# Attention: the logarithm of each row's sum joins its maximum in the by-key pass

## The reference

```
h = layernorm(x, gamma1, beta1)
q, k, v = h @ Wq + bq, h @ Wk + bk, h @ Wv + bv
scores = q @ k.T / sqrt(32), masked above the diagonal
context = softmax(scores) @ v
attention = context @ Wo + bo
```

## Time and profile before

| | |
|---|---|
| time, median of 3 runs | 1732.72 us (1732.4 to 1734.18) |
| profiled execution, first to last instruction | 1732.7 us |
| TensorE busy | 1657.8 us, 96% |
| VectorE busy | 1174.8 us, 68% |
| ScalarE busy | 977.3 us, 56% |
| GpSimd busy | 437.3 us, 25% |
| TensorE in the chain that ended last | 77% |
| mean granted TensorE clock | 0.980 |

### The profile page before, as it was taken

One profiled execution on the slowest core, in us unless ns is written; L12 is line 12 of the kernel. 1 busy time (PEld: TensorE's weight loads), 2 busy tenths in 40 slices (PEclk: granted clock), 3 DMA queues, 4 the chain that ended last, 5 costly groups with the idle time before them and its releaser, 6 DMA issues.

```text
span 1732.7 us, 27454 instructions
## 1 busy us (share of the span) xinstructions
PE 1657.8 (96%) x9416; PEld 1331.5 (77%) x9416; DVE 1174.8 (68%) x2758; ACT 977.3 (56%) x2258; POOL 437.3 (25%) x670
## 2 busy tenths in 40 slices
PE   6799988899999999999999899999999999999999
PEld 4688766667676777767777568888999999999998
DVE  6799775777777767685867737767565656565643
ACT  5788753777676767676767654634242424242422
POOL 5788530323132313223231212010101010101010
PEclk8899998999999999999999989999999999999999
DMA  7122233443444434344433524576646464646451
GB/s 308 51 97 79 92 122 97 99 99 93 116 100 117 99 97 125 81 123 99 99 88 85 183 104 170 209 279 241 243 170 243 170 243 170 244 170 243 171 195 67
DMA packets 61826, 254.81 MB, mean 147 GB/s; under 512 B 10580, under 2 KB 15956, under 8 KB 45944
## 3 DMA queue, kind: packets, MB, share of 16 engines
q1 hardware_dynamic: 61688, 253.06, 44.8%
HBM read 153.93 MB, written 48.23 MB: 117 GB/s over the span
## 4 chain that ended last, share of the span: by engine, by line
PE 77%; DVE 9%; ACT 4%; DMA 4%; SPq 2%; issue 2%; POOL 1%; DVEq 0%; POOLq 0%; ACTq 0%
PE psum L82 21%; PE psum L83 20%; PE psum L84 20%; PE psum L1632 4%; PE psum L1660 3%; PE psum L1613 3%; SPq L920 2%; DVE psum L1165 2%; PE psum L1538 2%; ACT psum L1408 1%; DMA k_stack<-k_samples 1%; DMA k_raw<-in_w_in 1%; DVE k_tokens L1216 1%; DVE k_samples L1206 1%; PE psum L1556 1%
## 5 line engine op out<-in xcount | busy, mean ns | idle before, releaser
L1408 ACT ACTIVATE psum<-psum,b_mx 128x512 f32<-128x512 f32 (+3 forms) x512 | 259.1, 507 | 199.4 <-DVE b_mx L1165 197.2
L1165 DVE CUSTOM_DVE_ANT_0 psum<-psum,b_mask 128x512 f32<-128x512 f32 (+3 forms) x512 | 244.4, 504 | 141.8 <-PE psum L1613 141.0
L2489 ACT ACTIVATE k_act<-k_stack_f,k_smalls 128x512 f32<-128x512 f32 x112 | 81.0, 723 | 336.5 <-DVE k_stack_f L2277 336.5
L1418 ACT ACTIVATE k_exps<-psum 128x512 f32<-128x512 f32 (+1 forms) x384 | 204.1, 533 | 20.6 <-PE psum L1632 18.7
L1632 PE MATMUL psum<-k_stack 98*128 98x512 f32 (+3 forms) x512 | 159.3, 353 | 16.5 <-ACT k_exps L1418 16.2
L2130 POOL TENSOR_SCALAR k_result<-k_result,k_pb 128x512 f32<-128x512 f32 x32 | 59.9, 1886 | 448.4 <-DVE k_result L2196 448.4
L2256 DVE TENSOR_TENSOR k_act_lo<-k_act,k_act_hi 128x512 fp32r<-128x512 f32 x112 | 77.3, 691 | 130.9 <-ACT k_act_hi L2492 130.8
L1613 PE MATMUL psum<-k_stack 96*128 96x512 f32 (+3 forms) x512 | 150.1, 335 | 2.5 <-ACT psum L1408 2.5
L82 PE MATMUL psum<-k_act_hi,k_w_hi 128*128 128x512 f32 x384 | 150.9, 393 | 0.6 <-DVE k_act_lo L2256 0.6
L83 PE MATMUL psum<-k_act_lo,k_w_hi 128*128 128x512 f32 x384 | 150.7, 392 | 0.0
L84 PE MATMUL psum<-k_act_hi,k_w_lo 128*128 128x512 f32 x384 | 150.4, 392 | 0.0
(11 more groups left out here) (368 smaller groups left out, 4563.7 us busy)
## 6 DMA issues: line engine op xcount, KB each, us to landing
k_stack<-w_factors SPq DMA_DIRECT2D x35, 1792.0 KB, 8.0
k_stack<-k_samples SPq DMA_DIRECT2D x384, 128.0 KB, 2.4
k_weights<-w_factors SPq DMA_DIRECT2D x17, 1792.0 KB, 7.6
x<-k_tokens SPq DMA_DIRECT2D x10, 1024.0 KB, 4.1
k_tokens<-x SPq DMA_DIRECT2D x8, 1024.0 KB, 5.0
d<-k_result SPq DMA_DIRECT2D x32, 256.0 KB, 2.5
k_raw<-x SPq DMA_DIRECT2D x8, 1024.0 KB, 4.8
k_raw<-d SPq DMA_DIRECT2D x8, 1024.0 KB, 7.0
```

The source lines that it names most:

```text
L1165: last = dve.tensor_tensor_reduce(got, got, mask[:, S - width:S], -INV_SQRT_DH, -2.0 * MASKED, ALU.add, ALU.min, mx[n % 2][:, h, t:t + 1])
L1408: act.activation(sc(n, u)[:, at:at + width], sc(n, u)[:, at:at + width], ACT.Exp, bias=mx[n % 2][:, h, t:t + 1], scale=-1.0, accum_out=sum ...
L1418: act.activation(exps[n % 2][:, h, at:at + width], by_key(n, u)[:, 0:width], ACT.Exp, scale=INV_SQRT_DH).then_inc(k_act, 1)
L2489: act.activation(act_f[:], whole_tile, ACT.Gelu, bias=small(smalls, "b1", 2 * pair % M + second)).then_inc(pair_gelu, 1)
```

## The change

The row sum's logarithm is subtracted from `mx` once the exponentials by query of a half are done. The by-key pass then gives exp(score - maximum - log(sum)), which is the softmax itself, and the context needs no scaling. ScalarE takes the logarithm of a half (`log_sums`, 128x8), VectorE subtracts it (`shift_rows`, 128x8), and only then does TensorE transpose the half. The second half's transpose and its split move from step 1 to step 2, on VectorE behind `qk_out`. The reciprocal, its spread, its four transposes, the piece "bc" and `over_sums` are gone. ScalarE rounds the context to its high part straight from PSUM, in step 6 instead of 7, and VectorE takes the low part from the PSUM bank in step 7. The transpose of the first half waits for that low part, since it writes the same bank.

```
@@ bank_uses: "bc" is gone from each list @@
-    bc = [("bc", *divmod(n - 2, G), "dve")] if 0 <= n - 2 < GROUPS else []
@@ VectorE @@
-        def invert(n):
-            dve.wait_ge(e_act, exps_until(n, UNITS - 1))
...
-            dve.reciprocal(recs[:], sums[n % 2][:]).then_inc(rec_set, 1)
-
-        def over_sums(n):
...
-            dve.tensor_tensor(ctx_at(n), ctx_at(n), pj(name), ALU.mult).then_inc(pj_dve, 1)
+        def shift_rows(n, half):
+
+            dve.wait_ge(log_set, 2 * n + half + 1)
+            both = two_heads(mx[n % 2], half)
+            dve.tensor_tensor(both, both, two_heads(logs, half), ALU.subtract).then_inc(shift_set, 1)
 
         def ctx_low(n):
             dve.wait_ge(ch_set, n + 1)
-            dve.tensor_tensor(low_at(n), ctx_at(n), ch[:, n % G, :].bitcast(F32), ALU.subtract).then_inc(cl_set, 1)
+            dve.tensor_tensor(low_at(n), ctx_bank, high_at(n).bitcast(F32), ALU.subtract).then_inc(cl_set, 1)
...
             if u == 1 and 0 <= n - 1 < GROUPS:
-                maxima_out(n - 1, 1)
-                invert(n - 1)
+                shift_rows(n - 1, 1)
+            if u == 7 and 0 <= n < GROUPS:
+                shift_rows(n, 0)
+            if u == 7 and 0 <= n - 2 < GROUPS:
+                ctx_low(n - 2)
             if u == 8 and 0 <= n < GROUPS:
                 maxima_out(n, 0)
             if u == 2 and 0 <= n + 1 < GROUPS:
                 qk_out(n + 1, 0)
-            if u == 8 and 0 <= n - 2 < GROUPS:
-                over_sums(n - 2)
-            if u == 10 and g != 2 and 0 <= n - 2 < GROUPS:
...
+            if u == 2 and 0 <= n - 1 < GROUPS:
+                maxima_out(n - 1, 1)
@@ ScalarE @@
-        def context_out(n):
+        def log_sums(n, half):
+
+            act.wait_ge(e_act, exps_until(n, UNITS // 2 * (half + 1) - 1))
+            if n:
+                act.wait_ge(shift_set, 2 * n + half - 1)
+            act.activation(two_heads(logs, half), two_heads(sums[n % 2], half), ACT.Ln).then_inc(log_set, 1)
+
+        def ctx_high(n):
             wait_context(act, n, CTX_ORDER[-1])
...
-            act.activation(ctx_at(n), ctx_bank, ACT.Copy).then_inc(ctx_out, 1)
+            act.activation(high_at(n), ctx_bank, ACT.Copy).then_inc(ch_set, 1)
...
-            if u == 7 and 0 <= n - 2 < GROUPS:
-                context_out(n - 2)
+            if u == 6 and 0 <= n - 2 < GROUPS:
+                ctx_high(n - 2)
...
+                if n == 0:
+                    act.preload_act_table_set("natural_log_exp_and_others")
...
                         exponentials(*last)
+                        if last[1] in (UNITS // 2 - 1, UNITS - 1):
+                            log_sums(last[0], last[1] // (UNITS // 2))
@@ TensorE @@
-            pe.wait_ge(s_dve, UNITS * n + UNITS // 2 * (half + 1))
+            pe.wait_ge(shift_set, 2 * n + half + 1)
...
                 if n >= 2:
-                    pe.wait_ge(ctx_out, n - 1)
+                    pe.wait_ge(cl_set, n - 1)
...
-            if u == 7 and 0 <= n - 2 < GROUPS:
-                recs_back(n - 2)
...
-                    if u == 1 and 0 <= n - 1 < GROUPS:
+                    if u == 2 and 0 <= n - 1 < GROUPS:
                         maxima(n - 1, 1)
```

More of the change, by code:

```diff
@@ L771, in bank_uses @@
     if g == 0:
-        return qk + each("st", b + 1, range(J), "dve") + bc + v + after_back
+        return qk + each("st", b + 1, range(J), "dve") + v + after_back
     if g == 1:
-        return qk + each("tin", b + 1, range(T), "act") + bc + v
+        return qk + each("tin", b + 1, range(T), "act") + v
     if g == 2:
-        return qk + each("tb", b + 1, range(J), "act") + bc + each("wo", b - 1, range(J - 1), "dve")
-    return qk + each("wo", b - 1, (J - 1,), "dve") + after_in + v[:2 * (n < 0)] + bc + each("p", b + 2, (0,), "dve") + v[2 * (n < 0):]
+        return qk + each("tb", b + 1, range(J), "act") + each("wo", b - 1, range(J - 1), "dve")
+    return qk + each("wo", b - 1, (J - 1,), "dve") + after_in + v[:2 * (n < 0)] + each("p", b + 2, (0,), "dve") + v[2 * (n < 0):]
 PJ, PJ_TAKEN, _taken = {}, [], {"act": 0, "dve": 0}
@@ L826, in attention_engines @@
     max_hi, max_lo = (keep["maxima"][DH * k:DH * k + 2 * T, :] for k in range(2))
-    sums, recs = [sb(f"sums{k}", [P, HG, T]) for k in range(2)], sb("recs", [P, HG, T])
+    sums, logs = [sb(f"sums{k}", [P, HG, T]) for k in range(2)], sb("logs", [P, HG, T])
+    two_heads = lambda a, half: a[:, 2 * half:2 * half + 2, :]
     st, mv = sb("st", [P, T, 6]), sb("mv", [P, T, 2])
@@ L1059, in slots @@
                     prepare_rstd(AFTER)
[L1060 to L1063, removed]
         return ahead, slots
@@ L1268, in beside @@
                 qk_out(n + 1, 0)
-            if u == 8 and 0 <= n - 2 < GROUPS:
-                over_sums(n - 2)
-            if u == 10 and g != 2 and 0 <= n - 2 < GROUPS:
-                if g == 3:
-                    ctx_low(n - 3)
-                ctx_low(n - 2)
+            if u == 2 and 0 <= n - 1 < GROUPS:
+                maxima_out(n - 1, 1)
             if u in (9, 11) and g == 2 and present(b - 1):
@@ L1596, in wo_piece @@
             out = claim(name) if g == 0 else pj(name)
-            last = three_pass(pe, out, [(w_hi["wo"][:, g, at], w_lo["wo"][:, g, at], ch[:, g, :], low_at(G * b + g))],
+            last = three_pass(pe, out, [(w_hi["wo"][:, g, at], w_lo["wo"][:, g, at], high_at(G * b + g), low_at(G * b + g))],
                               start=g == 0, stop=g == G - 1)
@@ L1654, in context @@
                 else:
-                    pe.wait_ge(ctx_out, n)
+                    pe.wait_ge(cl_set, n)
                 wait_cut(pe, n)
@@ L1663, in context @@
             last.then_inc(v_done, 1)
-        def recs_back(n):
-            pe.wait_ge(rec_spread, n + 1)
-            out = claim(("bc", *divmod(n, G)))
-            for t in range(T):
-                last = pe.transpose(out[:, t * P:(t + 1) * P], rec_rows[:, t, :, :].rearrange("p h d -> p (h d)"), ident[:])
-            last.then_inc(pj_full, 1)
         def pieces_at_turn(n):
```

29 lines of the change are left out of this document (6 added, 23 removed).

## The result

The changed kernel takes 1741.81 us, the median of 6 runs (1738.78 to 1747.11); the kernel before, run beside it, took 1734.32 (1732.4 to 1736.83). The ratio is 1.005, 95% interval 1.0035 to 1.0064: slower by half a per cent, 7.5 us. The forecast was 1741, slower by 8.3. The profiled execution is the slowest of the six: its time is 1747.11 us, 5.3 above the median, and its span, first to last instruction, 1745.3. So its parts differ from the profile of before (span 1732.7) by 12.6 us and not by 7.5. A span is no time: where a run of this case has both, the time is 1.7 to 1.9 us longer, so it was chance that the span of before equalled the median of its first three runs. The forecast started from that median, 1732.7; over six runs it is 1734.32, 1.6 us more.

A forecast was written before the change was run, and what follows sets the result against it. TensorE, busy 1657.8 of 1732.7 us, was taken as the bound, running close behind VectorE and ScalarE in steps 5 to 8. Ordinary samples +5.4, chain places +4.8 and last slots -1.5 gave +8.7: 1741, range 1727 to 1757.

The forecast's parts named there:

- (1): Second-half maxima split behind VectorE's projection pair: step 3's row maximum 0.6 us late, 0.4 in first slot; fourth-slot stall 0.35.
- (2): Context's bank freed later, by VectorE in step 7; with (1), first slot +0.35, second +0.5, fourth +0.45 us.
- The sum: Whole kernel: six ordinary samples +5.4, eight chain places +4.8, last slots -1.5; together +8.7 us, stated as 1741.
- The ordinary sample: Four slots of the attention stage, 90.27 us before: forecast 0.35 + 0.5 - 0.4 + 0.45 = +0.9 us.
- The long places: Eight places where stacked rows' DMA, VectorE's pair and row maximum are the chain: 0.6 us each in full, +4.8.
- The signs: Trace marks of being right: VectorE's order, transposes waiting for k_cl, samples of 91 to 92.5 us, no table loads between slots.
- What goes: Work removed: four reciprocal transposes, 0.45 us a slot, 14.4 over 32 slots; also over_sums (0.688), reciprocal, spread and cast.
- What comes: Work added per slot: two ScalarE logarithms, 0.2 us each, and two VectorE subtractions, 158 ns for a like one; by themselves hidden.
- rivals' table case: Exponential and logarithm need different ScalarE tables, two loads per logarithm: 164 us more, 1897; chance 0.01.
- (3): Third slot: second output product no longer waits for over_sums, 0.5 us less; net -0.4 us.
- The covers: Rival: VectorE and ScalarE regain their losses in steps 9 to 11, TensorE keeps its savings: 1720.4 us; chance 0.18.
- every lateness adds up: Rival: lateness reaches the bank's release undiminished in each slot and delays the next slot's rows: +18, 1750 us; chance 0.25.

The follow-up runs named there:

- (1) alone: Kernel before with only the second half's transpose and split moved from step 1 to step 2, behind the projection pair: 1745.08 us, ratio 1.007.
- the changed kernel without (2): Changed kernel with the context's old way out: ScalarE copies it in step 7, VectorE takes the low part in step 10; 1735.21 us, ratio 1.0018.
- the filler: Kernel before plus one unread 448-column VectorE statistic per slot behind the projection pair of step 2, nothing moved: 1740.05 us, ratio 1.0031.
- the version with the late transpose: Changed kernel with both reorderings undone and the first-half maxima's transpose behind the by-key score of step 8: 1723.64 us, ratio 0.9939.

## Why the prediction was right, step by step

**The direction, and orders as the cause.** Right, and shown: undoing (1) and (2) turns +0.5% into -0.57%, and (1) alone makes the old kernel 0.7% slower.

**The sum.** It came within 1 us of the median, and that is partly luck: the base was 1.6 us too low, a median of three runs, and the difference 0.8 to 1.2 us too large (8.3 as stated, 8.7 as summed, against 7.5). The ordinary sample was given +0.9 and took +0.86 to +0.97 (90.27 to 91.13 and 91.24); that term is right in size. The long places were given +4.8. In the five samples measured, 8.0 us more stand against 5 x 0.9 = 4.5 of that kind, so 3.5 fell to the long ones, where six of the eight places had been given 3.6. But most of it came another way: one of the 0.6 us is seen in the chain as forecast, while a third sample was long, 2.3 us or more, which had no term; that the two sums agree is luck. The first sample, from the first score to its first steered-sum piece, was given no term of its own and took 80.1 us instead of 77.1: +3.0. TensorE's waiting there is 10.0 us against 10.5 before, so the 3 us are no added waits but busy time at a lower granted clock (0.82 instead of 0.88). The sum had no term for the clock. Measured from the steered-sum piece ahead of it, this stretch takes 85.5 us before (0.88), 88.1 in the changed kernel (0.83) and 88.1 in the kernel before with (1) alone (0.85); in the other versions it takes 84.1 to 86.5 (0.86 to 0.88), also in the changed kernel without (2), which has (1). With one profile of each, the cause stays open. The remainder, from the last such piece to the end, was 0.6 us longer, where -1.5, the last two places and some of the ordinary lateness had been given; 1.1 us more stand ahead of the first score, in stages that the change doesn't touch. All these parts are of the slowest of six runs, 5.3 us above the median.

**The signs.** The order on VectorE, the transposes that wait for `k_cl` and the absent table loads are as forecast; so are the ordinary samples, but only two of the five are ordinary. TensorE's idle time in the attention stage (277.5 to 1010 us before, 278.6 to 1022 now) grew by 18 us, against 20 forecast. Its busy time was to fall by 8 to 14 us and fell by 4.0: 7.2 less in the five samples, but 3.5 more in the first, at the lower clock, and 2.9 more ahead of the first score.

**What goes.** This term failed in size. 14.4 us was called the whole possible gain on TensorE, at 0.45 us in each of 32 slots; the chain has them at 23 places, 11.5 us. Three of the four transposes gave 3 us (0 to 5.7), and nothing in ordinary samples: what else would have held the next piece up there isn't shown. VectorE's relief of over_sums, which the sum had only in the third slot and at the end, gave 6 in the old kernel. That the changed one spends it again on the low part in step 7, and so within the price of (2), is argued and not shown.

**What comes.** 0.209 and 0.177 us, where 0.2 and 0.158 were taken. "Hidden" was nearly right: 0 to some 10 us together, 4 by the medians. By the rivals' table case they would have cost 164; no load stands between the slots. The Trainium skill, page "ScalarE: Activation LUTs", section "Table sets: the hidden batching unit", states that one named set holds both functions; the trace agrees, with 64 logarithms of 209 ns between exponentials and no load.

**(1).** The mechanism was right in both parts, the size too small. I gave it a stall of 0.35 us in the fourth slot, lateness that reached the transposes, and the 0.6 at eight places; it costs 10.6 to 13 us, by three comparisons. Missing was the score by query, which waits for the bank of the exponential behind the late row maximum (8 waits became 19 with (1) alone, 11 in the changed kernel). VectorE's 0.6 us alone are about 5.4 of it, by the filler; the rest goes with the split's own lateness, and the waits that only the moved split brings are those for the context's bank and the maxima's DMAs. How the two paths share it isn't shown: with the row maximum of step 3 relieved and the split later still, the price stayed (1.0075).

**(2).** Right: 5.5 us by the one comparison, 8 by the other (0.46% of 1733). The transpose that waits for `k_cl` is what the prediction asked to see, 14.2 us in 16 waits. When it moved behind the next score the price fell from 0.46% to 0.19%, a fall within the uncertainty.

**(3).** The third slot's gain was not tried by itself.

**The rivals.** The covers did not hold. That every lateness adds up was too dark by 8 us. The slower case came true, with (1) costing more than it was given. "The small instructions cost more than their rows", named as what could make it wrong, isn't shown: 0 to some 10 us for rows of 24.8.

**What stays open.** Why a sample is long: in such samples some batches of six stacked rows' DMAs are issued in 4.2 to 5.5 us instead of 3.9, and then DMA, pair and row maximum are the chain; but in the kernel before, such batches at 574 us (5.07) and 596 us (4.60) made no sample long. The versions with less for VectorE to do or with one transpose have none above 91.3 us among these five. I have not found what lengthens the issue.

## What to carry to other kernels

Ask of every small instruction that a change moves what is queued behind it, not what it costs: a small transpose and 0.6 us of VectorE's work one step later cost 12 us here, about as much as the 10 us that the change gives in its best order. An engine's share of the chain, like its waits, is no price: two pieces of this chain, 11.5 and 7.0 us, were worth about a third and about the whole of their share by the medians. Try it by shrinking the work alone. Read the granted clock before putting a longer stretch down to waits. If a change mixes work removed with an order altered, build the halves apart before giving up on it: this one loses 0.5% as made and gains 0.6% with its two orders undone.

## What the runs showed that I had not expected

Cutting one VectorE pass from 512 to 32 columns gained 0.36% in a kernel whose TensorE is busy for 96% of the span and VectorE for 68%. A full TensorE can still be fed late, and the average of the stage doesn't show it. And waits that end with one releaser may go on with another: 10 us fewer of TensorE's waits for the subtraction, in the version with the late transpose, changed the time by 0.04%, which is nothing that these runs can tell.
